# A gated cross-attention block on one core: projections in other slots of a hand-written order, and two normalising steps at other places

## The chip, the cores and the metric

The kernel runs on one core of a Trainium2 chip. Its engines are TensorE (PE, matmuls), VectorE (DVE), ScalarE (ACT), GpSimd (POOL) and SyncE (SP, which here only issues DMAs). The metric is the device time of one execution in microseconds (us); the program is launched once and its time is that of its one core.

## What is computed

The reference, cut to what matters:

```python
x = x + tanh(g_xattn) * xattn(layernorm(x), ctx, Wq, bq, Wkv, bkv, Wo, bo)   # x 4x256x512, ctx 4x1601x512
x = x + tanh(g_ffn) * ffn(layernorm(x), base_W, router_W, lora_A, lora_B)    # top 2 of 8 experts, rank 16

def xattn(query, kv, ...):               # 32 heads of 128, 8 key/value heads, 4 query heads on each
    q = (query @ Wq + bq)                # 256 x 4096
    k, v = split(kv @ Wkv + bkv)         # 1601 x 1024 each
    attn = softmax(q k^T / sqrt(128))    # per head 256 x 1601
    return (attn v) @ Wo + bo
```

All of it is float32. Matmuls run in a 32-bit format with fewer bits, so each factor is split into a high part and a low rest (`qh`, `ql`, `kh`, `kl`, ...), and a product is three matmuls: high by high, high by low, low by high.

## The kernel before

**Units and slots.** A unit `U` (0 to 63) is two heads of one batch entry, so 16 units make a batch entry `b`. Its queries are one moving matrix of 512 columns (2 heads x 256), and the 1601 keys are 13 tiles `t` of at most 128. One step of the program, a slot `s = 13*U + t`, holds one score tile of unit U (three matmuls into `psS`), and the tail of the unit before, which follows 16 to 19 slots behind: POOL subtracts the column maximum (`SUB` = 16, line 731), ACT takes the exponential twice, in full and as high part `ph` (`EXP` = 17, lines 884 and 887), DVE forms the rest `pl` and adds up the denominators (lines 947 and 1156), and PE multiplies by the values (`VAL` = 19, lines 544 to 546, "pv" below). Below, "slot 7 of unit 34" is s = 13*34 + 7.

**The order by hand.** All other work of PE is placed by the table `AT`, one row for each U % 4, thirteen words for the thirteen slots: `m` and `b` turn and spread the maximum, `s` and `r` turn the sum and spread its inverse, `o0` and `o1` are the output projection of unit U-2, `q0` and `q1` the query projections for unit U+1 (12 matmuls of 256 columns each), `k0` to `k3` a key projection in four pieces, `v0` to `v12` a value projection in thirteen, `x0` and `x1` turn the normalised x of the next batch entry (in units 14, 30 and 46). Each engine's program is written out in slot order and runs in that order. In slot s PE does the scores, the pv and then the jobs of s. ACT does the copy of the scores to `xs` (line 795), the two exponentials, the jobs' high parts (`qh` line 811, `kh` line 800, `vh`), and in slot 8 after these `oh` (line 919), the high part of the normalised attention output. DVE does the running maximum `mrun` (line 1132), in slot 8 the division by the sum (line 1137), in slot 9 `ol` (line 1141), then the rests of the jobs of slot s-1 (`ql` line 970, `kl` line 958, `vl`), then `pl` and the sum. `o0` stands in slot 10 and waits for `ol`.

**Banks.** Jobs and pv share the four 2 KB banks of `psW` in a ring: `take` hands out the bank that came free first in program order and waits for what empties it. For a projection that is DVE's rest (`s_ql`, `s_kl`, `s_vl`), for `r` the copy to `rbc`. pv of one unit holds a bank from slot 6 to slot 10 of the unit after the next, so that in slots 6 to 9 two banks are held by pv, and the jobs there take the other two in turn.

**POOL.** From unit 16 on the first three tiles of a unit are "lead" tiles: POOL makes their `pl` (line 735, steps L0, L1, L2 of `steps_at`), in slots 5, 6 and 7 of the next unit but in order with the subtractions S0 to S12; PE's pv of slots 6, 7 and 8 wait for them (`s_lp`). In batch entry 0 (units 0 to 15) only the first tile is a lead tile, and POOL also splits the weights and the context into high and low (`cut`, lines 722 and 724), whose order is set by `cuts`. For the next batch entry's x POOL runs two `tensor_scalar` (line 783) in unit 14, 30 or 46.

**The inverse deviation.** `floored_var` and `inverse_dev` (five small DVE instructions, lines 1002 to 1006, each waiting for the one before) with the square root `root` on ACT between them (line 827) make the factor of the second layernorm for six of eight tiles, in unit 60 or 61.

Of the kernel before, what the change touches and what calls it, by code (L numbers as in the profile page):

```python
# [18 lines left out]
def gated_block(nc: bass.Bass, x, ctxT, gx, gf, wq, bq, wk, wv, bkv, wo, bo, bw, rw, la, lb,  # L19
# [7 lines left out]
    B, LQ, D, LK = 4, 256, 512, 1601  # L27
    KT = D // 128
    LKP = LK + 1
    NT = (LK + 127) // 128  # L30
    CH = [(0, 384), (384, 384), (768, 384), (1152, 450)]
    NU = 16
    UN = B * NU
# [5 lines left out]
    NQ = B * LQ // 128  # L39
# [10 lines left out]
    def lead(U):  # L50

        return 1 if U < NU or U == UN - 1 else 3
# [2 lines left out]
    jobs = {s: [] for s in range(SLOTS)}  # L55
    AT = [
# [4 lines left out]
    ]  # L61
    for U in range(UN + 2):
# [18 lines left out]
    def halves(kind, n):  # L81
        return [(kind, n, a) for a in range(2 if kind in "vo" else 1)]
# [4 lines left out]
    cuts = {s: [] for s in range(SLOTS)}  # L87
    cuts[0] += halves("q", 2) + halves("q", 3)
    spare = [("c", n, 0) for n in range(16)]
    for U in range(NU + 1):  # L90
        at, u = NT * U, U % 4
        if U + 2 < NU:
            cuts[at + 7] += halves("q", 2 * U + 4)
            cuts[at + 8] += halves("q", 2 * U + 5)
        if u % 2 == 0 and U // 2 + 1 < 8:
            cuts[at + 9] += halves("k", U // 2 + 1)
        if u == 3 and U // 4 + 1 < 4:
            for a in range(2):
                cuts[at + 9 + a].append(("v", U // 4 + 1, a))
        if U != 1:  # L100
            for a in range(2):
                cuts[at + (12 if u == 3 or U == 0 else 13) + a].append(("o", max(U - 1, 0), a))
        for t in (9, 11) if u == 1 else (11,) if u != 3 or U == 3 else ():
            if spare:
                cuts[at + t].append(spare.pop(0))
    for n in range(16, 16 * (B - 1)):
        b, i = divmod(n, 16)
# [6 lines left out]
    stage, there, s = [], [[] for _ in range(4)], 0  # L114
    for no, (p, at) in enumerate(cut_at):
# [5 lines left out]
        if no >= len(first) + 2:  # L121
            s = max(s, at - 10, cut_at[last][1] + 1)
# [7 lines left out]
    with ExitStack() as ctx:  # L130
        def sb(name, shape, dt, c=ctx):
            return c.enter_context(nc.sbuf_tensor(name, shape, dt))
# [61 lines left out]
        x1 = sb("x1", [128, NQ - 2, 512], F32)  # L194
# [94 lines left out]
        def f32(ap):  # L289
            return ap.bitcast(F32)  # L290
# [14 lines left out]
        def steps_of(a, z, n):  # L305
            return steps[:, 8 * n + a:8 * n + z]
# [15 lines left out]
        for T in range(TN):  # L322
            U, t = divmod(T, NT)
# [370 lines left out]
        def _(eng):  # L694
# [46 lines left out]
            def merge(U):  # L741
                total = psum_[:, U % 2, :]
                pool.wait_ge(s_a, a_count[NT * U + NT - 1])
                pool.wait_ge(s_ap, 2 * (U - NU) + 1)
                eng.tensor_tensor(total, pp[:, 0, :], total, ALU.add).then_inc(s_ap)
# [8 lines left out]
            for s in range(SLOTS):  # L754
                U, t = divmod(s - SUB, NT)
                if 0 <= U < UN:
                    for step in steps_at[0 if lead(U) == 1 else 1][t]:
                        if step == "M" and U > 0 and lead(U - 1) == 3:
                            merge(U - 1)
                        if step in "M-":  # L760
                            continue
                        {"S": take_off, "L": lower_p, "A": add_p}[step[0]](NT * U + int(step[1:]))
                for p in cuts[s]:
                    cut(*p)
                if s == 2:
                    pool.wait_ge(s_bo, 16)
                    pool.wait_ge(s_tg, 1)
                    eng.tensor_scalar(xraw[:, :], xraw[:, :], tg[:, 0:1], None, ALU.mult).then_inc(s_bob)
                if s in (4, 13, 21, 28):
                    r = (4, 13, 21, 28).index(s) + 1  # L770
                    pool.wait_ge(s_bob, 1)
                    pool.wait_ge(s_acc, 16 * r)
                    if r < 4:
                        pool.wait_ge(s_bs, 2 + 2 * r)
                    for i in range(2):
                        eng.tensor_tensor(acc[:, i, :], acc[:, i, :], xraw[:, :], ALU.add).then_inc(s_bias)
                U, t = divmod(s, NT)
                b, u = divmod(U, NU)
                if u == 14 and t == 5 and b + 1 < B:
                    pool.wait_ge(s_stat, 1)  # L780
                    pool.wait_ge(s_x, 32 * (b + 1))
                    for i, raw in ((2 * b + 2, xraw[:, :]), (2 * b + 3, f32(cst[:, :]))):
                        eng.tensor_scalar(raw, raw, mv[:, i, 0:1], rstds[:, i:i + 1], ALU.subtract, ALU.mult).then_inc(s_xn)
                if s == TN - 8:
                    pool.wait_ge(s_k, 4 * NK)
                    pool.wait_ge(s_v, 52 * B)
                    for e in range(E):
                        eng.memset(rev[:, e:e + 1], float(E - e)).then_inc(s_rev)

        @block.scalar  # L790
        def _(eng):
# [33 lines left out]
            def root(n, a, z):  # L825
                act.wait_ge(s_ve, n)
                eng.activation(steps_of(a, z, 2), steps_of(a, z, 1), ACT.Sqrt).then_inc(s_sq)
# [32 lines left out]
            for s in range(SLOTS):  # L860
                if s < TN:
                    t = s % NT
# [6 lines left out]
                if 0 <= T < TN:  # L869
                    U, t = divmod(T, NT)  # L870
# [43 lines left out]
                if s % NT == 8 and 0 <= V < UN:  # L914
# [3 lines left out]
                    u = V % NU  # L918
# [2 lines left out]
                    upper_ctx(2 + s // 2)  # L921
                if s == 24:
                    root(2, 2, NQ)
                if s == NT * (UN - 3) + 1:
                    root(3, 0, NQ - 2)
                if s == TN - 1:
                    route(1)
# [9 lines left out]
        def _(eng):  # L937
# [3 lines left out]
            def settle(ins):  # L941
                done[0] += 1
                ins.then_inc(s_d)
                dve.wait_ge(s_d, done[0])
# [44 lines left out]
            def stats(i, src):  # L989
                turned[0] += 1  # L990
                eng.bn_stats(steps[:, 32:38], src).then_inc(s_bs)
                dve.wait_ge(s_bs, turned[0])
                settle(eng.bn_aggr(mv[:, i, :], steps[:, 32:38]))

            def floored_var(a, z):
                eng.tensor_scalar(steps_of(a, z, 1), mv[:, a:z, 1], EPS, None, ALU.add).then_inc(s_ve)
# [120 lines left out]
            for s in range(SLOTS):  # L1117
                U, t = divmod(s, NT)
                b, u = divmod(U, NU)
# [39 lines left out]
                if s in (4, 13, 21):  # L1159
                    r = (4, 13, 21).index(s) + 1  # L1160
# [9 lines left out]
                if u == 2 and t == 0 and 1 <= b < B:  # L1170
                    for i in range(2):
                        dve.wait_ge(s_acd, 32 * b)
                        stats(2 * b - 2 + i, acc[:, i, :])
                if s == NT * (UN - 3):
                    floored_var(0, NQ - 2)
                if s == NT * (UN - 3) + 3:
                    inverse_dev(3, 0, NQ - 2)
                if s == TN - NT:
                    dve.wait_ge(s_x1, 16)
# [72 lines left out]
```

## Time and profile before

| | us |
|---|---|
| median of three runs | 2353.43 (2351.94 to 2354.57) |
| the profiled execution, its time | 2350.98 |
| span of its trace | 2348.9 |

The profiled execution spends 2.1 us outside the span that the trace shows. In the page of the profile part 1 gives the busy time of each engine, part 4 the chain of work that ended last, followed back to the start and summed by engine. PE is busy for 97% of the span, but matmuls are pipelined: one of 512 columns is shown 0.39 us long though the next starts 0.23 us later. So an idle time of PE in the trace is some 0.16 us shorter than what was lost. In the timeline a row is start, duration, engine, line, operation, output<-inputs, shapes, count, and in brackets the idle time of the engine before it and what ended it.

### The profile page before, as it was taken

To read this page: it belongs to the slowest core of one execution; us is meant where nothing else is said; L and a number is where in the kernel's file an instruction comes from. 1 tells how busy PE (TensorE), PEld (TensorE's weight loads), DVE (VectorE), ACT (ScalarE), POOL (GpSimd) and SP (SyncE) were. 2 spreads that over 40 slices of the span, in tenths; PEclk is the share of its full clock that TensorE was granted. 3 is DMA by queue.
4 is the path that set the end of the run, shared out by engine and by line. 5 is a ranking of instruction groups with operands and counts; after the bars stand their busy time and mean duration, and the time that the engine had idled before them with its cause. 6 is when DMAs were issued, how large, how long until landed. Compare 5 with 4: busy or idle time off the path is not lost.

```text
span 2348.9 us, 37753 instructions
## 1 busy us (share of the span) xinstructions
PE 2285.9 (97%) x12568; PEld 1956.9 (83%) x12568; DVE 1827.6 (78%) x3167; ACT 1688.0 (72%) x3208; POOL 1621.9 (69%) x1367
## 2 busy tenths in 40 slices
PE   7999999999999999999999999999999999999988
PEld 6888888888888888888888888888788888888764
DVE  5887888879778787877778778787778768778775
ACT  4776777767777776776767777776777767777663
POOL 5896987977667786775757777774865757665651
PEclk9999999999999999999999999999999999999999
DMA  7444334463133233334223243324323222122211
GB/s 255 150 146 139 124 125 142 134 208 142 46 124 113 99 115 104 110 102 172 73 91 109 72 131 114 104 89 137 130 72 108 73 79 84 44 92 73 81 37 54
DMA packets 122591, 258.11 MB, mean 110 GB/s; under 512 B 13344, under 2 KB 46624, under 8 KB 122144
## 3 DMA queue, kind: packets, MB, share of 16 engines
q1 hardware_dynamic: 122400, 255.71, 32.2%
q8 instruction: 102, 1.67, 0.3%
q14 instruction: 89, 0.73, 0.1%
HBM read 188.81 MB, written 66.86 MB: 109 GB/s over the span
## 4 chain that ended last, share of the span: by engine, by line
PE 85%; DVE 6%; POOL 3%; issue 3%; ACT 2%; DMA 0%; SPq 0%; ACTq 0%; POOLq 0%; DVEq 0%
PE psW L362 13%; PE psW L363 12%; PE psW L364 12%; PE psW L544 7%; PE psS L362 7%; PE psS L364 7%; PE psS L363 7%; PE psW L546 7%; PE psW L545 7%; PE psW L417 2%; PE psW L425 2%; POOL xs L731 2%; DVE mrun L1132 2%; PE psW L462 1%; DVE pl L947 1%
## 5 line engine op out<-in xcount | busy, mean ns | idle before, releaser
L731 POOL TENSOR_TENSOR xs<-xs,mb 128x512 f32<-128x512 f32 (+1 forms) x832 | 1066.0, 1310 | 545.6 <-ACT mb L795 545.6
L1132 DVE TENSOR_TENSOR mrun<-psS,mrun 128x512 f32<-128x512 f32 (+1 forms) x704 | 484.3, 688 | 387.1 <-ACT xs L795 382.6
L795 ACT ACTIVATE xs<-psS 128x512 f32<-128x512 f32 (+1 forms) x832 | 497.7, 598 | 218.0 <-PE psS L364 208.6
L887 ACT ACTIVATE ph<-xs 128x512 fp32r<-128x512 f32 (+1 forms) x832 | 520.6, 626 | 0.0
L947 DVE TENSOR_TENSOR pl<-psP,ph 128x512 fp32r<-128x512 f32 (+1 forms) x674 | 461.1, 684 | 54.1 <-ACT ph L887 48.4
L1156 DVE TENSOR_TENSOR psum_<-psP,psum_ 128x512 f32<-128x512 f32 (+1 forms) x674 | 458.9, 681 | 0.0
L884 ACT ACTIVATE psP<-xs 128x512 f32<-128x512 f32 (+1 forms) x674 | 403.5, 599 | 1.7 <-DVE psum_ L1156 1.7
L362 PE MATMUL psS<-ql,kh 128*128 128x512 f32 (+1 forms) x832 | 344.8, 414 | 4.6 <-DVE mrun L1132 3.2
L544 PE MATMUL psW<-ph,vh 128*128 128x512 f32 (+1 forms) x832 | 335.8, 404 | 9.6 <-POOL pl L735 5.8
L546 PE MATMUL psW<-ph,vl 128*128 128x512 f32 (+1 forms) x832 | 328.1, 394 | 0.0
L545 PE MATMUL psW<-pl,vh 128*128 128x512 f32 (+1 forms) x832 | 328.1, 394 | 0.0
L364 PE MATMUL psS<-qh,kl 128*128 128x512 f32 (+1 forms) x832 | 327.5, 394 | 0.0
L363 PE MATMUL psS<-qh,kh 128*128 128x512 f32 (+1 forms) x832 | 327.5, 394 | 0.0
L362 PE MATMUL psW<-wvl,ch 128*128 128x256 f32 (+1 forms) x832 | 239.6, 288 | 2.7 <-DVE vl L947 2.7
L363 PE MATMUL psW<-wvh,ch 128*128 128x256 f32 (+1 forms) x832 | 234.2, 281 | 0.0
L364 PE MATMUL psW<-wvh,cl 128*128 128x256 f32 (+1 forms) x832 | 233.7, 281 | 0.0
L544 PEld LDWEIGHTS psW<-ph,vh 128*128 128x128 f32 (+1 forms) x832 | 156.4, 188 | 61.1 <-DVE pl L947 12.5
L795 ACT ACTIVATE vh<-psW 128x256 fp32r<-128x256 f32 (+1 forms) x208 | 80.3, 386 | 151.7 <-PE psW L364 149.8
L546 PEld LDWEIGHTS psW<-ph,vl 128*128 128x128 f32 (+1 forms) x832 | 156.4, 188 | 38.1
L545 PEld LDWEIGHTS psW<-pl,vh 128*128 128x128 f32 (+1 forms) x832 | 157.0, 189 | 36.3 <-issue 1.7
L364 PEld LDWEIGHTS psS<-qh,kl 128*128 128x128 f32 (+1 forms) x832 | 153.0, 184 | 38.8
L362 PE MATMUL psW<-cl,wkh 128*128 128x384 f32 (+1 forms) x512 | 178.0, 348 | 4.5 <-DVE cl L947 4.5
(155 smaller groups left out, 4557.3 us busy)
## 6 DMA issues: line engine op xcount, KB each, us to landing
wqh<-scr_wq SPq DMA_DIRECT2D x96, 256.0 KB, 2.6
wql<-scr_wq SPq DMA_DIRECT2D x96, 256.0 KB, 2.9
woh<-scr_wo SPq DMA_DIRECT2D x48, 512.0 KB, 3.2
wol<-scr_wo SPq DMA_DIRECT2D x48, 512.0 KB, 4.3
scr_wq<-wqh SPq DMA_DIRECT2D x32, 256.0 KB, 2.0
scr_wq<-wql SPq DMA_DIRECT2D x32, 256.0 KB, 2.5
scr_wo<-woh SPq DMA_DIRECT2D x16, 512.0 KB, 2.6
scr_wo<-wol SPq DMA_DIRECT2D x16, 512.0 KB, 4.2
```

The costliest lines, as they stand in the source:

```text
L362: eng.matmul(o, lh, rl, start=first, stop=False)
L363: eng.matmul(o, lh, rh, start=False, stop=False)
L364: return eng.matmul(o, ll, rh, start=False, stop=last)
L544: eng.matmul(o, vh[0:rows, t, hs], hi, start=t == 0, stop=False)
L545: eng.matmul(o, vh[0:rows, t, hs], lo, start=False, stop=False)
L546: eng.matmul(o, vl[0:rows, t, hs], hi, start=False, stop=t == NT - 1).then_inc(s_pv)
L731: eng.tensor_tensor(tile, tile, mb[0:rows_of(t), U % 2, :], ALU.subtract).then_inc(s_sub)
L795: return eng.activation(hi, src, ACT.Copy)
L887: eng.activation(ph[0:rows, T % RP, :], xs[0:rows, T % RX, :], ACT.Exp).then_inc(s_h)
L947: return eng.tensor_tensor(lo, src, f32(hi), ALU.subtract)
L1132: eng.tensor_tensor(run, psS[0:rows, s % 2, :], a, ALU.max).then_inc(s_m)
L1156: eng.tensor_tensor(total, p, total, ALU.add).then_inc(s_a)
```

## The change

It changes two rows of the table `AT`: in row 1 (units 1, 5, 9, ... 61) `v7` goes from slot 9 to slot 7 and `v8` from slot 10 to slot 9; in row 2 (units 2, 6, ... 62) `q1` goes from slot 6 to slot 8, behind `r` instead of ahead of it. The `cuts` for batch entry 0 follow: in units 2, 6 and 10 the split of the second query weight goes from slot 8 to 9, that of the key weight from 9 to 8. x's normalising on POOL goes from slot 5 to slot 6 of units 14, 30 and 46. The floored variance goes from slot 0 of unit 61 to slot 7 of unit 60, the root from slot 1 of unit 61 to slot 9 of unit 60, and the inverse deviation from slot 3 to slot 0 of unit 61.

```diff
     AT = [
         "m q0 b k3 q1 s v0 r v1 v2 o0 v3 o1",
-        "m,v4 v5 b,q0 v6 k0 s q1 r k1 v7 o0,v8 v9 o1,v10",
-        "m,v11 k2 b,v12 q0 k3 s q1 r - x0 o0 x1 o1",
+        "m,v4 v5 b,q0 v6 k0 s q1 r,v7 k1 v8 o0 v9 o1,v10",
+        "m,v11 k2 b,v12 q0 k3 s - r q1 x0 o0 x1 o1",
         "m q0 b k0 q1 s k1 r - k2 o0 - o1",
     ]
...
         if U + 2 < NU:
             cuts[at + 7] += halves("q", 2 * U + 4)
-            cuts[at + 8] += halves("q", 2 * U + 5)
+            cuts[at + (9 if u == 2 else 8)] += halves("q", 2 * U + 5)
         if u % 2 == 0 and U // 2 + 1 < 8:
-            cuts[at + 9] += halves("k", U // 2 + 1)
+            cuts[at + (8 if u == 2 else 9)] += halves("k", U // 2 + 1)
...
-                if u == 14 and t == 5 and b + 1 < B:
+                if u == 14 and t == 6 and b + 1 < B:
                     pool.wait_ge(s_stat, 1)
                     pool.wait_ge(s_x, 32 * (b + 1))
...
-                if s == NT * (UN - 3) + 1:
+                if s == NT * (UN - 3) - 4:
                     root(3, 0, NQ - 2)
...
+                if s == NT * (UN - 3) - 6:
+                    floored_var(0, NQ - 2)
                 if s == NT * (UN - 3):
-                    floored_var(0, NQ - 2)
-                if s == NT * (UN - 3) + 3:
                     inverse_dev(3, 0, NQ - 2)
```

**PE, unit 37, slot 7** (every fourth unit reads so). The first three rows are the slot's pv, L425 is `r`, and what follows it is what the change puts there. Before, the scores of slot 8 follow:

```order
L544 MATMUL psW<-ph,vh 128x512
L545 MATMUL psW<-pl,vh 128x512
L546 MATMUL psW<-ph,vl 128x512
L425 MATMUL psW<-ident,rinv 128x128 x4
L362 MATMUL psS<-ql,kh 128x512
L363 MATMUL psS<-qh,kh 128x512
L364 MATMUL psS<-qh,kl 128x512
```

Of the change:

```order
L544 MATMUL psW<-ph,vh 128x512
L545 MATMUL psW<-pl,vh 128x512
L546 MATMUL psW<-ph,vl 128x512
L425 MATMUL psW<-ident,rinv 128x128 x4
L362 MATMUL psW<-wvl,ch 128x256
L363 MATMUL psW<-wvh,ch 128x256
L364 MATMUL psW<-wvh,cl 128x256
```

The value projection `v7` (12 such rows) now stands directly behind `r`, ahead of the scores of slot 8, and takes the bank that `q1` had in slot 6.

**ACT, unit 38, slots 7 and 8.** `rbc` is the copy of the spread inverse sum, `qh` the high part of `q1`, `oh` that of the attention output; the `qh` of before stands three rows above the first row shown. Before:

```order
L795 ACTIVATE rbc<-psW 128x512
L795 ACTIVATE xs<-psS 128x512
L884 ACTIVATE psP<-xs 128x512
L887 ACTIVATE ph<-xs 128x512
L919 ACTIVATE oh<-psW,bkv_sb 128x512
L795 ACTIVATE xs<-psS 128x512
```

Of the change:

```order
L795 ACTIVATE rbc<-psW 128x512
L795 ACTIVATE xs<-psS 128x512
L884 ACTIVATE psP<-xs 128x512
L887 ACTIVATE ph<-xs 128x512
L811 ACTIVATE qh<-psW,bq_sb 128x256
L919 ACTIVATE oh<-psW,bkv_sb 128x512
L795 ACTIVATE xs<-psS 128x512
```

`qh`, which waits for PE's `q1`, now stands directly ahead of `oh`. On DVE `ql` moves likewise, from ahead of the division (line 1137) to behind `ol`.

**POOL, unit 30, slots 5 to 7.** The `pl` rows are the lead tiles' steps L0, L1 and L2, `xs` the subtractions, L783 x's normalising. Before:

```order
L735 TENSOR_TENSOR pl<-psum_,ph 128x512
L731 TENSOR_TENSOR xs<-xs,mb 128x512
L783 TENSOR_SCALAR xraw<-xraw,mv,rstds 128x512
L783 TENSOR_SCALAR cst<-cst,mv,rstds 128x512
L735 TENSOR_TENSOR pl<-pp,ph 128x512
L731 TENSOR_TENSOR xs<-xs,mb 128x512
L735 TENSOR_TENSOR pl<-pp,ph 128x512
```

Of the change:

```order
L735 TENSOR_TENSOR pl<-psum_,ph 128x512
L731 TENSOR_TENSOR xs<-xs,mb 128x512
L735 TENSOR_TENSOR pl<-pp,ph 128x512
L731 TENSOR_TENSOR xs<-xs,mb 128x512
L783 TENSOR_SCALAR xraw<-xraw,mv,rstds 128x512
L783 TENSOR_SCALAR cst<-cst,mv,rstds 128x512
L735 TENSOR_TENSOR pl<-pp,ph 128x512
```

The two instructions moved from between L0 and L1 to between L1 and L2.

## Rows read from the trace of the kernel before

**Rows 1.** The page, part 1 and the first line of part 4.

```profile
PE 2285.9 (97%) x12568; PEld 1956.9 (83%) x12568; DVE 1827.6 (78%) x3167; ACT 1688.0 (72%) x3208; POOL 1621.9 (69%) x1367
...
PE 85%; DVE 6%; POOL 3%; issue 3%; ACT 2%; DMA 0%; SPq 0%; ACTq 0%; POOLq 0%; DVEq 0%
```

**Rows 2.** Waits of the whole span: engine line <- releaser: us, times, longest.

```profile
PE psW L362 <- issue: 14.9, 12, 3.0
...
PE psW L544 <- POOL pl L735: 5.8, 5, 2.3
...
PE psS L362 <- DVE mrun L1132: 3.2, 1, 3.2
...
PE psW L362 <- DVE vl L947: 2.7, 15, 0.2
```

**Rows 3.** Timeline, unit 37: slot 7 into 8, and `v8` in slot 10.

```profile
1332.47 0.48 PE L362 MATMUL psS<-ql,kh 128*128 128x512 f32 x1
...
1332.86 0.48 DVE L970 SCALAR_TENSOR_TENSOR ql<-psW,bq_sb,qh 128x256 fp32r<-128x256 f32 x1
...
1341.53 0.41 DVE L947 TENSOR_TENSOR vl<-psW,vh 128x256 fp32r<-128x256 f32 x1
...
1342.00 0.39 PE L362 MATMUL psW<-wvl,ch 128*128 128x256 f32 x1 [0.18 <-DVE vl L947]
```

**Rows 4.** Timeline, unit 9, slot 7 into 8.

```profile
347.50 0.48 PE L362 MATMUL psS<-ql,kh 128*128 128x512 f32 x1
...
348.12 0.47 DVE L970 SCALAR_TENSOR_TENSOR ql<-psW,bq_sb,qh 128x256 fp32r<-128x256 f32 x1
```

**Rows 5.** Timeline, unit 34, slots 6 to 10, engine by engine.

```profile
1230.19 0.28 PE L362 MATMUL psW<-xtl,wqh 128*128 128x256 f32 x1
...
1231.49 0.28 PE L364 MATMUL psW<-xth,wql 128*128 128x256 f32 x1
...
1231.81 0.48 ACT L811 ACTIVATE qh<-psW,bq_sb 128x256 fp32r<-128x256 f32 x1 [0.48 <-PE psW L364]
...
1232.10 1.31 POOL L735 TENSOR_TENSOR pl<-pp,ph 128x512 fp32r<-128x512 f32 x1
...
1236.71 0.69 ACT L919 ACTIVATE oh<-psW,bkv_sb 128x512 fp32r<-128x512 f32 x1 [0.55 <-DVE psW L1137]
1237.29 0.59 ACT L795 ACTIVATE xs<-psS 128x512 f32<-128x512 f32 x1
...
1238.53 0.74 DVE L1141 SCALAR_TENSOR_TENSOR ol<-psW,bkv_sb,oh 128x512 fp32r<-128x512 f32 x1
...
1239.37 0.47 PE L362 MATMUL psW<-wol,oh 128*128 128x512 f32 x1 [1.09 <-issue]
```

**Rows 6.** Timeline, unit 10, slot 8, DVE.

```profile
389.31 0.47 DVE L970 SCALAR_TENSOR_TENSOR ql<-psW,bq_sb,qh 128x256 fp32r<-128x256 f32 x1
```

**Rows 7.** Timeline, unit 30, slots 6 to 10, POOL and PE.

```profile
1086.56 2.07 POOL L783 TENSOR_SCALAR xraw<-xraw,mv,rstds 128x512 f32<-128x512 f32 x1
...
1090.67 1.26 POOL L735 TENSOR_TENSOR pl<-pp,ph 128x512 fp32r<-128x512 f32 x1
...
1091.98 0.50 PE L544 MATMUL psW<-ph,vh 128*128 128x512 f32 x1 [2.25 <-POOL pl L735]
...
1098.74 0.47 PE L362 MATMUL psW<-wol,oh 128*128 128x512 f32 x1
```

**Rows 8.** Timeline around unit 61, ACT, DVE, POOL; the last row is the end phase.

```profile
2160.89 1.28 ACT L827 ACT_TABLE_LOAD   x1
2162.19 0.21 ACT L827 ACTIVATE steps<-steps 128x6 f32<-128x6 f32 x1
...
2169.16 1.26 DVE L1003 TENSOR_TENSOR steps<-rstd 128x6 f32<-128x6 f32 x1
...
2165.91 1.31 POOL L731 TENSOR_TENSOR xs<-xs,mb 128x512 f32<-128x512 f32 x1 [14.36 <-ACT mb L795]
...
2330.16 0.16 DVE L1003 TENSOR_TENSOR steps<-rstd 128x2 f32<-128x2 f32 x1
```

## The prediction

> **What bounds the kernel now.** I read the page first: PE is busy for 97% of the span and is 85% of the chain that ended last [rows 1]. So only two things change the time: PE's work, which this change leaves as it is, and the short idle times of PE. The list of waits of the whole span names those [rows 2]. Fifteen times a value projection waits for DVE's `vl` (0.18 us each): that is `v8` in slot 10 of each fourth unit. Eleven of the twelve waits called "issue" are some 1.08 us, and belong to `o0` in slot 10 of units 14, 18, 22 and on; the trace shows the same 1.1 us in units 2, 6 and 10 under other names. Five waits of `pv` for POOL, 5.8 us, nearly all in units 30 and 46. One of 3.2 us for DVE's `mrun` in unit 61. The change goes at each of these. The timelines then show one unit of each kind, since the units repeat within 0.01 us.
>
> **Value projections (units 5, 9, ... 61).** What is removed: `v8` starts at 1342.00, when `vl` of `v7` has ended at 1341.53 + 0.41 = 1341.94 [rows 3]; so PE wakes 0.06 later. The idle of 0.18 cost about 0.35, since matmuls are shown 0.16 longer than their spacing, and the first matmul behind a wait loses another 0.1 (one of `pv` lasts 0.50 in [rows 7], where 0.39 is usual). The scores right behind `r` also lose 0.09 today (0.48 long rather than 0.39 [rows 3]); that too goes. With `v8` a slot earlier and `o0` between it and `v9`, the rest has time: I follow `vl` of `v8` to about a microsecond ahead of `v9`. Gain 0.35 + 0.09 + 0.09 = 0.53.
>
> What is added: `v7` now stands directly behind `r` in slot 7, where the scores of slot 8 start today, at 1332.47. It takes the bank of `q1`, which ran in slot 6, and this bank is free only when DVE has done `ql`: 1332.86 + 0.48 = 1333.34 [rows 3], PE at 1333.40. Nothing that the change does makes this `ql` earlier, since it stands behind `mrun` of slot 7, which needs that slot's scores. PE is idle for 0.93, and with the 0.10 of the first matmul 1.03 are lost. Net a loss of 0.50 in each of the twelve units 17 to 61: 6.0 us. In batch entry 0 DVE is busier and `ql` ends at 348.12 + 0.47 = 348.59, while `v7`'s place is at 347.50 [rows 4]: 1.15 + 0.10 - 0.53 = 0.72 lost, in three units (5, 9, 13) 2.2 us. Unit 1 has no old `pv` and a free bank: nothing.
>
> **The query projection (units 2, 6, ... 62).** `q1` takes 1.42 (1230.19 to 1231.49 and one spacing of 0.12) [rows 5]. Without it in slot 6, slot 7 starts at 1230.19, and `r` follows within a microsecond and a half. But `pv` of slot 8 needs POOL's lead step L2, whose place in POOL's queue is unchanged: it ends at 1232.10 + 1.31 = 1233.41 [rows 5]. PE could be there at about 1233.0, waits to 1233.46, loses 0.1, and needs 0.70 for it; `q1` starts at 1234.26 and its last matmul at 1235.56. On ACT `qh` starts 0.32 behind that (1231.81 to 1231.49 in the rows): 1235.88. `oh`, today at 1236.71, is queued behind it and starts 0.38 later (0.48 less the 0.1 by which ACT's rows overlap, as 1237.29 lies in `oh`): 1236.26. Behind `oh` are `xs` and through it `mrun` and `ol`, then `o0`: all keep their distances and move by 0.45. So `o0` starts at 1238.92 rather than 1239.37. The 1.4 us by which `q1` should fill the pause are mostly lost to new waits, of `r`, of `pv` for L2, and a rest at `o0`. Ten units (18 to 62 without 30 and 46): 4.5 us gained.
>
> In batch entry 0 there is no L2. There DVE runs without a pause from slot 6 to `ol`, and loses one `ql` (0.47, about 0.4 from start to start) ahead of it [rows 6]: 0.4 gained in units 2, 6 and 10, 1.2 us. In unit 14 `x0` takes another bank, so that `o0` gets `q1`'s and waits for `ql`, now behind `ol`: it gives the 0.4 back, 0. The two splits of weights that swap on POOL, and the loads of query weights on SP, which are issued two slots later in these units, both have more than ten slots to the next use.
>
> **x's normalising (units 30 and 46).** L1 waits for its input until 1086.83, 0.27 behind the place of the first L783 [rows 7]. Then come L1 and S4 (1.27 each from start to start) and the two L783 (2.05 each, as from 1086.56 to 1090.67): L2 starts at 1093.47 and ends at 1094.73, so `pv` of slot 8 starts at 1094.78. Today's wait of 2.25 in slot 7 goes, but one of over 4 us in slot 8 comes, and `q1`, which today is done before the wait, stands behind it. From there as above: `q1` at 1095.58, its last matmul at 1096.88, `qh` 1097.20, `oh` 1097.58, `ol` 1.82 later (1236.71 to 1238.53 in [rows 5]) at 1099.40, then `ql` 0.65 later, whose bank `o0` takes in these units: it ends at 1100.53. `o0` starts at 1100.59 rather than 1098.74 [rows 7]: 1.85 lost, twice, 3.7 us. The old wait is not removed but moved to a place where more is behind it.
>
> **The inverse deviation.** Today four of its five DVE instructions last 1.2 us each (L1003: 1.26), while POOL runs without a pause; in the end phase, with POOL idle, 0.16 [rows 8]. In slot 0 of unit 61 POOL is idle (14.36 us, to 2165.91), and DVE has nothing that is due, so the five take about 1.0 and delay `mrun` by under 0.7, which PE's next reader does not notice. The wait of 3.2 in unit 61 goes [rows 2]; with the 0.16 and 0.1 as above 3.4 are gained. Here the Trainium skill agrees (SBUF — State Buffer, section on the two separate sides): DVE and GpSimd share a port pair with an exclusive lock, and the loser blocks for the whole instruction. By its rule the early `floored_var`, among POOL's subtractions, could be held up to 1.3 as well; DVE would pass that on to `o0` of unit 60 as under 0.3.
>
> `root` moves from a place where ACT has slack to slot 9 of unit 60. Its table loads are 1.28 each, twice, with the next instruction 0.02 behind (2160.89 + 1.28 = 2162.17, 2162.19) [rows 8]. I follow ACT, 1.3 late, through slots 10 to 12, to `m` of unit 61, which still has some 0.2 us. Cost 0. The Trainium skill has a rule against this (ScalarE: Activation LUTs, "What ACT_TABLE_LOAD costs"): a drain of 1.38 on top of each load. As an estimate by that page ACT would be 2.8 later still, `m` would wait more than 2, and the sum would be higher by as much; the row shows no such gap.
>
> **Sum.** +6.0 +2.2 -4.5 -1.2 +3.7 -3.4 = +2.8 us. Profiled, 2350.98 + 2.8 = 2353.8; the median of before lies 2.45 above its profiled execution, so 2356.2, 0.12% slower. Less than 0.2% (4.7 us) is not told from no change by a measurement of this kernel.
>
> **Rivals.** *The sum stands* (0.50), give or take 3: fifteen, thirteen and two units repeat an error of 0.1 to 0.5 in a step.
> *`v7` does not wait* (0.08): if its bank were free, each of 15 units would gain 0.53: 2.8 - 8.2 - 8.0 = -13.4, 2340. For it: nothing but the short wait seen today; against it the order of the ring.
> *`q1` ahead of `oh` takes the whole gain* (0.19), the other side: where `pv` of slot 8 starts later than 1233.9, `oh` is no earlier than today. L2 is 0.45 short of that. Then the 5.7 gained in thirteen units are gone: +8.5, 2362.
> *x's normalising costs nothing more* (0.15), if `q1` and the x tiles find their banks and engines free: -3.7, so -0.9, 2352.5.
> *The root disturbs unit 60* (0.08): if ACT is held once more as long as the two loads take (2.56), less the 0.2 of slack, `m` waits 2.3: +5.1, 2358.5. It decides from 0.2 on. For it: ACT has three operations and a copy in each of the short slots 10 to 12; against it: the 0.02 behind the load. A drain behind each load, as that page of the Trainium skill has it, would act so.
>
> Faster by over 0.2%: the second and a little of the fourth, 0.11. Slower by over 0.2% (over 2358.1): the third, half of the fifth, and the upper end of the first, 0.29. Within: 0.60. The range 2350 to 2361.5 leaves out the second and a part of the third.
>
> **What would show it.** In the profile after: `v7` of slot 7 waiting for DVE `ql` some 0.75 us as PE's idle (0.93 less 0.16), fifteen times, and no 0.18 for `vl`; `o0`'s wait of 1.08 down to some 0.3, and new waits of `pv` for POOL of some 0.3 in slot 8 of ten units; one of over 4 us in units 30 and 46; L1003 at 0.16 and no wait for `mrun` in unit 61. The prediction is wrong if the first of these is missing, or if the units of row 2 of the table are shorter by 1 us or more.

## The result, and the profile after it

| us | before | after |
|---|---|---|
| median of 20 runs each | 2352.87 (2351.26 to 2355.86) | 2358.47 (2354.86 to 2370.14) |
| profiled execution | 2350.98 | 2357.18 |
| its span | 2348.9 | 2355.1 |
| mean granted clock of PE | 0.997 | 0.994 |

The ratio after to before is 1.0031, with a 95% interval of 1.0020 to 1.0042: 0.31% slower, some 7.3 us, which is also the difference of the two means (2360.3 and 2352.9; the medians are 5.6 apart). Five of the 20 executions after took 2367.3 to 2370.1; the other 15 took 2354.9 to 2360.5 and lie 4.6 above before in the mean. The traced one is one of the 15. The predicted time was 2356.2 in a range of 2350 to 2361.5. The span grew by 6.2 us, where the sum said 2.8.

The page after, part 1 and the first line of part 4, beside [rows 1]:

```profile
PE 2290.8 (97%) x12568; PEld 1961.3 (83%) x12568; DVE 1825.9 (78%) x3167; ACT 1687.3 (72%) x3208; POOL 1621.5 (69%) x1367
...
PE 88%; POOL 5%; DVE 4%; ACT 2%; issue 2%; DMA 0%; SPq 0%; ACTq 0%; POOLq 0%; DVEq 0%
```

PE has the same 12568 matmuls, but is busy for 4.9 us more: some of them took longer. That is the first hint at the term that was wrong. In the chain DVE fell from 6% to 4% and POOL rose from 3% to 5%.

Three rows of PE's waits over the whole span, beside [rows 2]:

```profile
PE psW L362 <- DVE ql L970: 11.6, 17, 0.9
PE psW L544 <- POOL pl L735: 11.3, 13, 4.3
...
PE psW L362 <- issue: 5.8, 11, 3.0
```

The `vl` waits (2.7 us) and the `mrun` wait (3.2) are gone, "issue" went from 14.9 to 5.8, and in their place are 11.6 for `ql` and 5.5 more for POOL.

The value projection in unit 37, PE and DVE on the timeline, beside [rows 3]:

```profile
1338.19 0.60 PE L425 MATMUL psW<-ident,rinv 128*128 128x128 f32 x4
...
1338.93 0.47 DVE L970 SCALAR_TENSOR_TENSOR ql<-psW,bq_sb,qh 128x256 fp32r<-128x256 f32 x1
...
1339.46 0.39 PE L362 MATMUL psW<-wvl,ch 128*128 128x256 f32 x1 [0.67 <-DVE ql L970]
```

`v7` waits for the `ql` that frees `q1`'s bank: it ends at 1339.40, and PE is there at 1339.46.

The query projection in unit 34 (which starts 6.57 us later here than in [rows 5]), POOL, PE, ACT and DVE, slots 7 to 10:

```profile
1238.65 1.31 POOL L735 TENSOR_TENSOR pl<-pp,ph 128x512 fp32r<-128x512 f32 x1
...
1240.01 0.50 PE L544 MATMUL psW<-ph,vh 128*128 128x512 f32 x1 [0.21 <-POOL pl L735]
...
1242.44 0.48 ACT L811 ACTIVATE qh<-psW,bq_sb 128x256 fp32r<-128x256 f32 x1 [0.97 <-PE psW L364]
1242.81 0.68 ACT L919 ACTIVATE oh<-psW,bkv_sb 128x512 fp32r<-128x512 f32 x1
...
1245.47 0.47 PE L362 MATMUL psW<-wol,oh 128*128 128x512 f32 x1 [0.28 <-issue]
```

`pv` waits 0.21 for L2, whose place in the unit has not moved (1238.65 less 6.57 is 1232.08; 1232.10 before). `oh` stands behind `qh`, and `o0`'s wait is down from 1.09 to 0.28. `o0` starts 0.47 earlier in the unit.

x's normalising in unit 30, beside [rows 7], POOL, PE, ACT, DVE and PE again:

```profile
1095.79 1.27 POOL L735 TENSOR_TENSOR pl<-pp,ph 128x512 fp32r<-128x512 f32 x1
...
1097.12 0.80 PE L544 MATMUL psW<-ph,vh 128*128 128x512 f32 x1 [4.32 <-POOL pl L735]
...
1098.14 0.63 PE L546 MATMUL psW<-ph,vl 128*128 128x512 f32 x1
1098.57 0.41 PE L362 MATMUL psW<-xtl,wqh 128*128 128x256 f32 x1
...
1101.37 0.47 ACT L811 ACTIVATE qh<-psW,bq_sb 128x256 fp32r<-128x256 f32 x1 [6.89 <-PE psW L364]
...
1104.86 0.47 PE L362 MATMUL psW<-wol,oh 128*128 128x512 f32 x1
```

The unit starts at 1069.89, and at 1067.57 before. L2 begins 25.90 us into it, as was predicted (1093.47 less 1067.57). But the matmuls behind it last 0.80 and 0.63 where 0.50 and 0.39 are usual, `q1` starts 28.68 into the unit rather than 28.01, and `o0` 34.97 rather than 33.02. The windows around the wait say why. Their columns are the window and its length, busy time and count of PE, PEld (PE's weight loads), DVE, ACT and POOL, the granted clock, the DMA share and GB/s:

```profile
1090.50:1097.10 6.60, 2.30 (x11) 1.36 (x10) 5.24 (x10) 3.98 (x8) 6.60 (x5) 0.84 0.75 274
1097.10:1101.30 4.20, 4.18 (x16) 3.89 (x17) 0.00 (x0) 0.00 (x0) 4.20 (x4) 0.50 0.00 0
1101.30:1105.00 3.70, 3.68 (x18) 2.74 (x17) 2.03 (x4) 3.63 (x8) 3.70 (x4) 0.93 0.45 142
```

Behind the wait the granted clock is 0.50, which is 1.2 GHz, for 4.2 us and some 0.5 us of the third window, and PE is without a pause in them. DVE and ACT have nothing to do meanwhile: they wait for this PE.

Last, unit 61 and the end of unit 60, ACT, DVE, and PE's next scores, beside [rows 8]:

```profile
2156.46 1.28 ACT L827 ACT_TABLE_LOAD   x1
2157.76 0.21 ACT L827 ACTIVATE steps<-steps 128x6 f32<-128x6 f32 x1
...
2168.80 0.17 DVE L1003 TENSOR_TENSOR steps<-rstd 128x6 f32<-128x6 f32 x1
...
2169.61 0.69 DVE L1132 TENSOR_TENSOR mrun<-psS,xs 128x512 f32<-128x512 f32 x1
...
2181.56 0.48 PE L362 MATMUL psS<-ql,kh 128*128 128x512 f32 x1
```

L1003 is down from 1.26 to 0.17, and no scores wait for `mrun`.

**Where the 6.2 us are.** The traces can be laid side by side unit by unit, from the first scores of a unit to those of the next (us; the middle columns are the length of one unit):

| units | before | after | sum, measured | sum, predicted |
|---|---|---|---|---|
| 17 to 57, every fourth (11) | 40.10 | 40.60 | +5.46 | +5.5 |
| 61: `v7`, and the inverse deviation | 43.55 | 40.59 | -2.96 | +0.5 - 3.4 |
| 5, 9, 13 | 40.10 | 40.82 | +2.14 | +2.2 |
| 18 to 62, every fourth but 30 and 46 (10) | 34.69 | 34.19 | -5.04 | -4.5 |
| 6, 10 and 14 | 34.94 (10) | 34.55 | -0.75 | -0.8 |
| 30 | 37.24 | 41.02 | +3.79 | +1.85 |
| 46 | 37.24 | 40.71 | +3.47 | +1.85 |

The other units and the two ends make +0.1 together. They hold parts that differ from trace to trace with no edit near them (unit 0 lasts from 28.4 us in e3 to 32.9 in e6; there are waits for weights and context in units 0 and 2), and they are left out of what follows; so is the 0.4 forecast for unit 2, which is 0.7 longer in this trace. All terms but one are met within 0.06 us a unit. Units 30 and 46 together cost 7.3 us instead of 3.7 (that the mean times differ by 7.3 as well is chance).

### The profile page after: what moved, and what is told of

Same layout as the page of the kernel before. It is cut to its first block, busy times and chain, and to the rows that moved or that the text cites. A ratio compares the mean times of both kernels' runs of the same rounds, so it can differ in the third digit from the quotient of the medians.

```text
span 2355.1 us, 37757 instructions
## 1 busy us (share of the span) xinstructions
PE 2290.8 (97%) x12568; PEld 1961.3 (83%) x12568; DVE 1825.9 (78%) x3167; ACT 1687.3 (72%) x3208; POOL 1621.5 (69%) x1367
## 4 chain that ended last, share of the span: by engine, by line
PE 88%; POOL 5%; DVE 4%; ACT 2%; issue 2%; DMA 0%; SPq 0%; ACTq 0%; POOLq 0%; DVEq 0%
PE psW L362 13%; PE psW L363 13%; PE psW L364 13%; PE psS L364 7%; PE psS L362 7%; PE psS L363 7%; PE psW L544 7%; PE psW L546 7%; PE psW L545 7%; POOL xs L731 2%; PE psW L417 2%; PE psW L425 2%; POOL pl L735 2%; PE psW L462 1%; DVE mrun L1132 1%
## 5 line engine op out<-in xcount | busy, mean ns | idle before, releaser
L800 ACT ACTIVATE kh<-psW,bkv_sb 128x384 fp32r<-128x384 f32 (+1 forms) x128 | 76.3, 596 | 145.2 <-PE psW L364 145.2
```

## The experiments

Each was timed in five rounds beside the kernel before. The unit lengths of the profiled executions, which carry most of the verdicts (u9 is unit 9 and stands for 5, 9, 13; u37 for 17 to 57; u34 for 18 to 58):

| | u9 | u34 | u37 | u30 | u46 | u61 | ratio to before, 95% |
|---|---|---|---|---|---|---|---|
| before | 40.10 | 34.69 | 40.11 | 37.24 | 37.24 | 43.55 | |
| after | 40.82 | 34.19 | 40.60 | 41.02 | 40.71 | 40.59 | 1.0031 (1.0020, 1.0042) |
| e1_v | 40.82 | 34.69 | 40.59 | 37.23 | 38.74 | 45.45 | 1.0033 (1.0021, 1.0044) |
| e2_q | 40.10 | 34.19 | 40.10 | 39.77 | 39.74 | 43.52 | 0.9992 (0.9983, 1.0001) |
| e3_root | 40.10 | 34.68 | 40.10 | 37.23 | 37.23 | 40.11 | 0.9967 (0.9954, 0.9979) |
| e4_x | 40.10 | 34.69 | 40.09 | 39.88 | 38.56 | 45.01 | 1.0009 (1.0000, 1.0018) |
| e5_split | 40.82 | 34.19 | 40.59 | 40.19 | 38.84 | 40.60 | 1.0034 (1.0016, 1.0051) |
| e6_xback | 40.82 | 34.18 | 40.59 | 40.69 | 39.92 | 40.61 | 1.0012 (0.9997, 1.0027) |
| e7_v7slot8 | 43.49 | 34.17 | 43.51 | 41.20 | 41.35 | 43.45 | 1.0219 (1.0198, 1.0239) |
| e8_v8late | 39.65 | 34.68 | 39.65 | 37.23 | 38.02 | 44.55 | 0.9971 (0.9958, 0.9984) |
| e9_best | 39.66 | 34.19 | 39.65 | 35.07 | 35.07 | 39.65 | 0.9916 (0.9900, 0.9933) |
| e10_xidle | 40.11 | 34.69 | 40.11 | 35.12 | 35.12 | 44.95 | 0.9975 (0.9964, 0.9985) |
| e11_longwait | 40.11 | 34.68 | 40.10 | 37.24 | 37.99 | 47.87 | 1.0012 (1.0003, 1.0021) |
| e12_after_xidle | 40.81 | 34.19 | 40.60 | 35.08 | 35.07 | 40.60 | 0.9977 (0.9965, 0.9989) |

The columns u9, u34 and u37 repeat to 0.02 us wherever the edit that bears on them is the same. Two columns do not: 46 has 37.24, 38.74, 37.23, 38.02 and 37.99 in five kernels that don't touch it (before, e1, e3, e8, e11), 61 has 43.55, 43.52, 45.01 and 44.95 in four (before, e2, e4, e10).

### The change in its four parts (e1 to e4)

Each is the kernel before with one part of the change. The value projections, alone:

```diff
-        "m,v4 v5 b,q0 v6 k0 s q1 r k1 v7 o0,v8 v9 o1,v10",
+        "m,v4 v5 b,q0 v6 k0 s q1 r,v7 k1 v8 o0 v9 o1,v10",
```

> The kernel before with the one row of the table for the value projections changed (v7 in slot 7, v8 in slot 9), nothing else. Theory (bank of q1): v7 waits for DVE's ql in each of 15 units, 1.03 us lost against 0.53 gained, 1.25 against 0.53 in batch entry 0: 12 x 0.50 + 3 x 0.72 = +8.2 us against before. Rival (the new order costs nothing and the wait of v8 goes): 15 x -0.53 = -8 us.

Measured: 2362.64 us, 1.0033; the units named are longer by 0.48 (11 of them, 5.38) and by 0.71 (2.13), as the prediction had it. The waits of PE name the cause:

```profile
PE psW L362 <- DVE ql L970: 10.7, 15, 0.9
```

The rival that `v7` doesn't wait is out. By the ratio this kernel is 7.8 us slower than before, where 8.2 were expected. But the span of its trace is 11.8 longer, and 2.9 of that come from nothing that the edit touches: 1.5 in unit 46 and 1.4 in unit 61 (45.45 less 43.55 and 0.50). More on that below.

The query projection, with the two lines of `cuts`:

```diff
-        "m,v11 k2 b,v12 q0 k3 s q1 r - x0 o0 x1 o1",
+        "m,v11 k2 b,v12 q0 k3 s - r q1 x0 o0 x1 o1",
```

> The kernel before with q1 in slot 8 of units 2, 6, ... 62 and the two swapped splits of weights; x's normalising stays in slot 5. Units without x: 10 x -0.50 and 3 x -0.4, -6.2 us. Units 30 and 46: without q1 ahead of it the pv of slot 7 waits for L1 some 3.8 us, then the pv of slot 8 some 0.7 us, and q1 behind: o0 about 1.55 us later by the queues alone, -6.2 + 3.1 = -3 us in all. If a wait of 3.8 us also halves the granted clock, as the one of 4.3 us in the changed kernel did, then 2 x 1.9 more, about +1 us. Rival (q1 ahead of oh takes the gain): no unit shorter, +3 us or more.

Measured: 2351.85, 0.9992. The ten units are shorter by 5.09, 6 and 10 by 0.81, 14 by nothing. So the rival "`q1` ahead of `oh` takes the whole gain" is out as well. Units 30 and 46 are 2.5 longer each, where 1.55 was expected of the queues: with x's normalising where it was, PE comes to its `pv` 1.4 us earlier and waits 3.7 rather than 2.3 for POOL:

```profile
PE psW L544 <- POOL pl L735: 9.8, 13, 3.7
```

The root and the inverse deviation:

```diff
-                if s == NT * (UN - 3) + 1:
+                if s == NT * (UN - 3) - 4:
                     root(3, 0, NQ - 2)
...
+                if s == NT * (UN - 3) - 6:
+                    floored_var(0, NQ - 2)
                 if s == NT * (UN - 3):
-                    floored_var(0, NQ - 2)
-                if s == NT * (UN - 3) + 3:
                     inverse_dev(3, 0, NQ - 2)
```

> The kernel before with the floored variance, the root and the inverse deviation at their new places, nothing else. Theory: the wait of 3.2 us in unit 61 goes and unit 60 is not longer: -3.4 us. Rival (the table loads hold ACT and then PE in unit 60): unit 60 or the start of 61 up to 2.3 us longer, -1 us.

Measured: 2347.37, 0.9967. Unit 61 is shorter by 3.44, and unit 60 stays at 33.59: the root disturbs nothing, and what the early `floored_var` costs does not reach PE. The time is 7.8 us below before by the ratio, over twice what was expected. The wait that is gone was followed by the lower clock in four of the six traces that have it, at 1.4 us each (below), which makes up for some 1 of the 4.4 in excess; the rest is not explained. The four L1003 of this kernel:

```profile
L1003 DVE TENSOR_TENSOR steps<-rstd x4: 161/164/1003, 8.3 to 2325.1; 128x2 f32<-128x2 f32 x2, 128x6 f32<-128x6 f32 x2
```

x's normalising:

```diff
-                if u == 14 and t == 5 and b + 1 < B:
+                if u == 14 and t == 6 and b + 1 < B:
```

> The kernel before with x's normalising in slot 6 rather than 5, nothing else. q1 still stands in slot 6, ahead of the wait. The pv of slot 7 no longer waits, that of slot 8 waits some 3.2 us for L2; o0 about 0.3 us later in units 30 and 46: +0.6 us, and no fall of the clock, since a wait of 3.2 us in unit 61 of the kernel before left it at full. Rival (the new place alone is what cost 3.5 us in each unit): +7 us.

Measured: 2356.48, 1.0009. This expectation failed. Unit 30 is longer by 2.64 and 46 by 1.31, where the queues give 0.3 each (`pv` of slot 8 starts 0.34 later in the unit than before). The wait moved to slot 8 and is 3.27 long; behind it the clock is at its lower level, and then at its upper one again:

```profile
1096.30:1099.60 3.30, 3.30 (x11) 2.57 (x10) 1.11 (x2) 1.64 (x3) 3.30 (x3) 0.50 0.00 0
1099.60:1103.50 3.90, 3.90 (x17) 3.20 (x16) 3.27 (x7) 2.24 (x4) 3.90 (x4) 0.88 0.02 4
```

The four ratios add up to 0.01% above before, and the change has 0.31%. By the unit lengths the parts do not fall short of the whole (unit 30: +2.53 and +2.64 alone, +3.79 together). The gap of some 7 us is as large as the two things that no trace shows: the 2.7 us by which the five executions of over 2367 us raise the mean of the changed kernel (7.3 less 4.6), and the 4.4 of e3. Each ratio is known to some 2 to 3 us only.

### Is it the clock behind the wait? (e5, e6, e10 to e12)

The theory now: what units 30 and 46 cost beyond 1.85 is PE at 1.2 GHz behind the wait. The rival is that the order of the queues is mis-followed there. The first experiment splits the two L783 between slots 5 and 6 of the changed kernel, so that the wait parts into two:

```diff
-                if u == 14 and t == 6 and b + 1 < B:
+                if u == 14 and t in (5, 6) and b + 1 < B:
...
-                    for i, raw in ((2 * b + 2, xraw[:, :]), (2 * b + 3, f32(cst[:, :]))):
+                    for i, raw in (((2 * b + 2, xraw[:, :]), (2 * b + 3, f32(cst[:, :])))[t - 5],):
```

> The changed kernel with x's first normalising instruction in slot 5 and the second in slot 6: the same work on POOL, L2 ends at nearly the same time (0.25 us earlier), but PE's one wait of 4.3 us is split into one of 1.8 in slot 7 and one of some 2.5 in slot 8. Theory (a wait of over 4 us halves the granted clock for the 4 us behind it): the clock stays at full, units 30 and 46 are 2.2 us shorter each, -4.4 us against the changed kernel. Rival (the loss is the queue alone, L2's place): -0.5 us.

Measured: 2357.58, 1.0034. The clock fell in one unit and not in the other. Windows of unit 30 (its wait, and behind it) and of unit 46 behind its wait:

```profile
1094.60:1099.10 4.50, 2.10 (x10) 1.43 (x10) 3.02 (x5) 2.43 (x5) 4.50 (x4) 0.96 0.76 276
1099.10:1102.00 2.90, 2.83 (x10) 2.55 (x11) 0.75 (x2) 0.00 (x0) 2.90 (x4) 0.50 0.01 4
...
1666.00:1669.00 3.00, 2.99 (x19) 2.72 (x20) 0.69 (x2) 0.56 (x2) 3.00 (x3) 1.00 0.00 0
```

One program, the same instructions and queues in both units: 40.19 us where the granted clock fell to 0.50 and 38.84 where it stayed at 1.00. The 1.35 between them is the clock alone. And 38.84 is what the queues give: 37.24 + 1.85 - 0.25 for the split (by the trace `pv` of slot 8 starts 0.32 earlier in the unit than in the changed kernel, which would make 38.77). So the prediction's 1.85 was the right price at 2.4 GHz, to within 0.1. The time did not fall by the 4.4 expected: units 30 and 46 are 0.83 and 1.87 shorter than in the changed kernel, but the first unit is 2.6 longer in this trace, and 5 of the 12 executions took 2364 to 2377.

Next, x's normalising back in slot 5, the rest of the change kept:

```diff
-                if u == 14 and t == 6 and b + 1 < B:
+                if u == 14 and t == 5 and b + 1 < B:
```

> The changed kernel with x's normalising back in slot 5. PE's wait is 3.8 us in slot 7 and 0.7 us in slot 8, L2 ends 0.3 us earlier. If a wait of 3.8 us leaves the clock at full: 2 x -2.2 = -4.5 us against the changed kernel; if it halves it: -0.6 us, with the slow matmuls in slot 7 and r instead of q1, perhaps less slow ones on the path.

Measured: 2355.85, 1.0012; units 30 and 46 shorter than in the changed kernel by 0.33 and 0.79. In both the clock falls behind their waits of 3.7, in unit 46 only 1.5 us after the end of the wait:

```profile
1664.10:1665.60 1.50, 1.50 (x9) 1.27 (x10) 0.00 (x0) 0.08 (x1) 1.50 (x2) 1.00 0.49 173
1665.60:1669.00 3.40, 3.39 (x11) 2.38 (x10) 1.76 (x3) 2.15 (x4) 3.40 (x4) 0.50 0.02 8
```

So of the 7.3 us of units 30 and 46 most is not due to the move of x's normalising, but to its standing anywhere near these slots once `q1` isn't ahead of it: e2 shows 5.0 of them.

Then a wait made longer with nothing else changed: in the kernel before, L1004 of the inverse deviation done three times instead of once, the same product written again.

```diff
+                for _ in range(2 if n == 3 else 0):
+                    settle(eng.tensor_tensor(t2, t1, ve, ALU.mult))
```

> The kernel before with one of the five small DVE instructions of the inverse deviation done three times instead of once in unit 61 (the same value is written): PE's one wait there goes from 3.2 to some 5.7 us. Theory (such a wait halves the granted clock behind it): unit 61 longer by 2.5 us of wait and 1.4 to 2 us of matmuls at half clock, +4 to +4.5 us in its trace. Rival (the clock has another cause, the lag is queueing): +2.5 us and no row at half clock.

Measured: 2357.14, 1.0012. Unit 61 is 4.3 us longer, though DVE's two more instructions (2.41 us) lengthen the wait by 2.4, from 3.16 to 5.58. The windows, the wait and then what is behind it, and under them the same place in the kernel before, where the wait is 3.2 and the clock stays:

```profile
2171.90:2177.60 5.70, 0.21 (x2) 0.00 (x0) 5.53 (x7) 0.75 (x2) 4.90 (x5) 0.79 0.00 0
2177.60:2181.70 4.10, 4.00 (x13) 3.46 (x14) 2.87 (x6) 1.63 (x3) 0.64 (x1) 0.50 0.00 0
```

```profile
2171.90:2175.00 3.10, 0.00 (x0) 0.02 (x1) 3.03 (x4) 0.49 (x1) 3.10 (x3) 1.00 0.00 0
2175.00:2178.00 3.00, 2.99 (x19) 2.59 (x20) 2.67 (x6) 1.64 (x3) 1.90 (x3) 1.00 0.00 0
```

In 4.1 us PE does 13 matmuls there, and 19 in 3.0 us at the full clock. What this shows is the price of the lower clock apart from the queues. That it came because the wait was longer is less certain from this run alone, since the clock also fell behind the wait of 3.2 in four of the six other traces that have it.

Last, the wait taken away. POOL is idle for more than 10 us early in units 30 and 46. x's normalising goes there, to slot 2, and the load of x that it needs starts a unit earlier; in unit 14 both stay. As e10 on the kernel before, as e12 on the changed one (there `t == 6` is what is replaced):

```diff
-                if u == 14 and t == 1 and b + 1 < B:
+                if (u, t) == ((13, 1) if b else (14, 1)) and b + 1 < B:
...
-                if u == 14 and t == 5 and b + 1 < B:
+                if u == 14 and t == (2 if b else 5) and b + 1 < B:
```

> The kernel before with only x's normalising of units 30 and 46 moved to that idle stretch of POOL. PE's waits for L1 and L2 go and o0's wait comes back in part: units 30 and 46 2.1 us shorter each, -4.2 us against before. Rival (the DMA of x or DVE's port now delays something): less than 2 us.

Measured: 2348.7, 0.9975; units 30 and 46 shorter by 2.12 each, as expected. Unit 61, untouched, is 1.4 longer in the profiled execution, and again it is the clock behind its 3.2 us wait:

```profile
2172.50:2175.60 3.10, 2.96 (x8) 2.44 (x9) 2.12 (x5) 1.31 (x3) 1.71 (x2) 0.50 0.00 0
```

> The changed kernel with x's normalising of units 30 and 46 in the idle stretch of POOL. Theory (PE's wait of 4.3 us and the half clock behind it are all that is wrong in these units): from 41.0 and 40.7 to about 34.9 us, -12 us against the changed kernel, so some 6 below before. Rival (q1 ahead of oh, with x0 beside it, costs as much): units of 37 us or more.

Measured: 2346.42, 0.9977, and 11.2 us less span than the changed kernel. Unit 30 is 5.94 shorter and unit 46 5.63; both last 35.08. POOL does its two L783 even before PE's unit starts (at 1070.53), and the second ends 19.5 us before L0 (the first `pl`), and `pv` of slot 8 has no wait; POOL, then PE:

```profile
1063.29 2.10 POOL L783 TENSOR_SCALAR xraw<-xraw,mv,rstds 128x512 f32<-128x512 f32 x1
1065.35 2.10 POOL L783 TENSOR_SCALAR cst<-cst,mv,rstds 128x512 f32<-128x512 f32 x1
...
1086.96 1.31 POOL L735 TENSOR_TENSOR pl<-psum_,ph 128x512 fp32r<-128x512 f32 x1
...
1096.59 0.40 PE L544 MATMUL psW<-ph,vh 128*128 128x512 f32 x1
```

With the wait gone, the queue's part and the clock's part are gone together.

### The value projections: another slot, and a version that beats both (e7 to e9)

If `v7` waits for `q1`'s bank, a slot later the bank should be free. On the changed kernel:

```diff
-        "m,v4 v5 b,q0 v6 k0 s q1 r,v7 k1 v8 o0 v9 o1,v10",
+        "m,v4 v5 b,q0 v6 k0 s q1 r v7,k1 v8 o0 v9 o1,v10",
```

> The changed kernel with v7 in slot 8 ahead of k1, one slot later: it still takes q1's bank, but ql has ended by then. Theory (the wait for the bank is the whole loss of these units): 12 x -1.03 and 3 x -1.25 = -16 us against the changed kernel, so about -9 us against before. Rival (another wait takes its place, for instance k1 or v8 for their banks): -8 us or less against the changed kernel.

Measured: 2408.33, 1.0219. This missed by far: the span is 41 us longer than the changed kernel's, and not 16 shorter. The wait for `ql` did go; one for `vl` came, in slot 9 of unit 37. DVE, then PE:

```profile
1367.23 0.69 DVE L1132 TENSOR_TENSOR mrun<-psS,mrun 128x512 f32<-128x512 f32 x1 [2.40 <-ACT xs L795]
1367.84 0.74 DVE L1141 SCALAR_TENSOR_TENSOR ol<-psW,bkv_sb,oh 128x512 fp32r<-128x512 f32 x1
1368.49 0.41 DVE L947 TENSOR_TENSOR vl<-psW,vh 128x256 fp32r<-128x256 f32 x1
...
1368.96 0.38 PE L362 MATMUL psW<-wvl,ch 128*128 128x256 f32 x1 [2.06 <-DVE vl L947]
```

and ACT ahead of them:

```profile
1365.55 0.58 ACT L800 ACTIVATE kh<-psW,bkv_sb 128x384 fp32r<-128x384 f32 x1 [1.73 <-PE psW L364]
1366.03 0.68 ACT L919 ACTIVATE oh<-psW,bkv_sb 128x512 fp32r<-128x512 f32 x1
1366.60 0.60 ACT L795 ACTIVATE xs<-psS 128x512 f32<-128x512 f32 x1
```

`k1` now follows `v7` on PE and so comes later; ACT's `kh` waits for it with `oh` and `xs` queued behind, DVE's `mrun` waits for `xs` with `ol` and `vl` queued behind, and `v8` needs `vl`'s bank. The expectation's rival had named a wait of `v8` for its bank, but nothing had been followed behind `kh`. All of the 15 waits of 2.1 us but one are followed by the lower clock:

```profile
1369.00:1372.90 3.90, 3.90 (x17) 3.46 (x18) 1.62 (x3) 0.96 (x3) 3.71 (x5) 0.64 0.30 105
```

The one is in unit 53, and that unit is 41.98 long; those where it fell have 43.5. So of the 2.9 us a unit 1.4 are the wait, and 1.5 the clock.

The other way is to leave `v7` in slot 9, and to move `v8` from slot 10 to slot 11, ahead of `v9`. On the kernel before:

```diff
-        "m,v4 v5 b,q0 v6 k0 s q1 r k1 v7 o0,v8 v9 o1,v10",
+        "m,v4 v5 b,q0 v6 k0 s q1 r k1 v7 o0 v8,v9 o1,v10",
```

> The kernel before with v8 moved from slot 10 to slot 11, ahead of v9, nothing else: vl of v7 is then long done. Theory (the 0.18 us of idle in the rows cost 0.44 us in each of 15 units): -6.6 us against before. Rival (they cost what the rows show): -2.7 us.

Measured: 2347.4, 0.9971. The units are shorter by 0.45 each, where 0.44 was expected (14 of them, 6.3 us together; unit 61 is 1.0 longer, with the lower clock behind its 3.2 us wait). So `vl` has time if `v8` stands a slot later, and `v7` need not come near `q1`'s bank.

The last kernel joins what held up: e8's row, the query projection and the root as in the change, and e10's x.

> The kernel before with v8 in slot 11 (the table's row otherwise as before), q1 in slot 8, the inverse deviation at its new place, and x's normalising for the last two batch entries in the stretch in which POOL waits for the next maximum (slot 2 of units 30 and 46, its load from slot 1 of units 29 and 45). Theory, if the parts add: -3.4 (root), -6.7 (v8), -5.9 (q1), -2.4 in each of units 30 and 46: -21 us against before. Rival (the parts share their slack): less than two thirds of it.

Measured: 2332.7 us (2330.7 to 2343.7), 0.9916 with an interval of 0.9900 to 0.9933: 0.84% faster than before, and by the two ratios 1.1% faster than the changed kernel. The span is 20.3 us shorter, where 21 were expected. PE's waits and POOL in unit 30, where x's two rows follow the last subtractions and 11.9 us of idle time are still left:

```profile
PE psW L362 <- issue: 5.8, 11, 3.0
...
PE psW L544 <- POOL pl L735: 3.2, 13, 0.5
```

```profile
1049.14 6.36 POOL L731 TENSOR_TENSOR xs<-xs,mb 128x512 f32<-128x512 f32 x5
1055.49 2.08 POOL L783 TENSOR_SCALAR xraw<-xraw,mv,rstds 128x512 f32<-128x512 f32 x1
1057.55 2.08 POOL L783 TENSOR_SCALAR cst<-cst,mv,rstds 128x512 f32<-128x512 f32 x1
1071.51 1.30 POOL L731 TENSOR_TENSOR xs<-xs,mb 128x512 f32<-128x512 f32 x1 [11.88 <-ACT mb L795]
```

The two longest waits of `pv` for POOL are down to 0.5, and between 100 us and 2250 us of the span no stretch of matmuls at the lower clock is left.

## Why the prediction was right, and which term was not

*The value projections.* The bank ring, the ending `ql` and the net loss of 0.50 and 0.72 a unit held: 0.50 and 0.71. `v7`'s idle is 0.67 (0.75 was said), fifteen times; the 0.18 for `vl` is gone. e1 has the same units alone. It was the largest term, and "`v7` does not wait" would have changed the sign.

*The query projection.* It gains 0.50 a unit rather than 0.45, and every wait along the way is there: `pv` for L2 0.21 (some 0.3 was said), `oh` behind `qh`, a rest of 0.28 at `o0` (0.3). Units 6, 10 and 14 came as predicted.

*The inverse deviation.* -3.46 against -3.4, in unit 61 alone, and e3 repeats it. L1003 lasts 0.17 while POOL is idle, and 1.26 before, while POOL ran. That is the port rule of the Trainium skill (SBUF — State Buffer, section on the two separate sides); the rows agree. The early `floored_var` (L996) among POOL's subtractions lasts 0.57 rather than 0.16, and unit 60 is no longer for it. The Trainium skill's rule on the drain at table loads (ScalarE: Activation LUTs, "What ACT_TABLE_LOAD costs") is not borne out in the new place either: the root's instruction starts at 2157.76, 0.02 behind the load (2156.46 + 1.28 = 2157.74), and unit 60 keeps its 33.59.

*x's normalising is the term that was mis-sized*: "1.85 lost, twice, 3.7 us", measured 7.3. The step that failed is "From there as above": it took the matmuls behind a wait of over 4 us to run as those of unit 34 do. L2 came at its place in the unit to 0.01 us and `pv` behind it to 0.02. Behind this wait PE got 1.2 GHz for 4.7 us in unit 30 and 3.4 in unit 46, which adds 1.9 and 1.6. That it is the clock and not the queue is shown by e5, where the one unit that kept the clock has the queue's price to within 0.1 us, by e11, where the wait was lengthened by itself and the unit grew by 1.9 more than the wait, and by e12, where all of it goes with the wait. The prediction has no term for the granted clock, whose mean is 0.997 before, and no window behind a wait. The waits of units 30, 46 and 61 in the before trace (2.3, 2.3 and 3.2 us) were followed by the full clock in that execution, and there was no longer one in the steady part to show it.

With the clock at 2.4 GHz the sum would have been +2.7 in the span; it was +6.2. So the time came out inside the range, but past the edge of 0.2% that the prediction gave a chance of 0.29: the same mechanisms, one of them dearer. Part of the distance has no mechanism at all yet: without the five executions of over 2367 us the mean is 4.6 us above before, just under that edge (4.7).

*Open.* Which of the shorter waits are followed by the lower clock is not settled. In units 30, 46 and 61 of the fourteen profiled executions it followed waits of 4.3 and 5.6 us each time (5 of 5) and those of 3.3 and 3.7 each time (6 of 6), but that of 3.2 us in unit 61 in 4 of 6, and that of 2.3 in unit 46 in 3 of 5 while never in unit 30. One fall costs 0.7 to 2.3 us (most in unit 30 of e4, 2.64 less 0.3). For the executions without a trace the mean granted clock is known, and it goes with the time: of the 25 of the kernel before that ran beside e9 to e12, the two at 0.997 took 2350.0 and 2350.3 us and the three at 0.993 took 2357.1 to 2357.6. So the clock can account for most of a spread of 7 us; where it fell in them is not shown. It does not explain the 5 of the 20 runs of the changed kernel that took 2367 to 2370: they have 0.991 to 0.993, and four others with 0.992 or 0.993 took 2358.4 to 2360.5. Such runs are not peculiar to the change: beside e5 to e8 the kernel before took 2363.4 to 2364.2 three times at a clock of 0.994, and 2354.3 to 2355.2 three times at the same. None of them has a trace. The parts of the start that vary (up to 4.5 us in unit 0) weren't looked into.

## What to carry to other kernels

A wait isn't gone when its job is moved a slot; ask which work has been put behind it, on every engine that queues (one `kh` made e7's span 41 us longer). A ring of buffers is part of the order: whoever moves a producer takes the buffer of another one, and its release sets the start. And a pause of the matmul engine can cost more than its length (here up to 2.3 us more, behind pauses of 2 to 6 us), so look at the granted clock behind each long wait, and put a helper engine's long jobs where that engine is idle, however far from their use.

## What the runs showed of the hardware

Behind eleven waits of 3.3 to 5.6 us PE's granted clock was 0.50 each time, for 2.9 to 5.8 us of the work behind the wait and although PE hardly paused in it, and then high again; 13 matmuls took 4.1 us in such a stretch, against 19 in 3.0 at the full clock (e11 and before). In some cases the fall came only 1.1 to 1.5 us behind the end of the wait (unit 30 of e2, unit 46 of e6), in others during it (unit 30 of the changed kernel, 2.1 us before its end). Waits of the same length, at the same place of a unit, had the fall in one trace and not in another (unit 46 with 2.3 us: in e1, e8 and e11, not in before and e3; unit 61 with 3.2 us: in e1, e4, e8 and e10, not in before and e2). The Trainium skill (TensorE: Matmul & The Clock Gate, Part 1: The HAM clock gate) names the same two levels, and says that how many matmuls run at the lower one at a kernel's start differs from run to run. The starts were not compared here; in the middle of a kernel the rows show that whether a stretch at the lower level comes behind a wait differs.
